# Values of all tokens projected token-major in the first stage of an attention block, and the nine projections that are left in a step in another order

## What is computed

```python
x = x + attn(layernorm(x), ...)
q = (h @ Wq.T).reshape(B, L, H, D)          # H = 32 heads, D = 128
k = (h @ Wk.T).reshape(B, L, KVH, D)        # KVH = 8 groups, 4 heads each
v = (h @ Wv.T).reshape(B, L, KVH, D)
q, k = rope(q), rope(k)
dt = softplus(h @ Win.T + dt_bias); g = dt * -exp(A_log_bias)
G = cumsum of g inside chunks of 128 tokens
y = (q k^T * decay(G)) (v dt)  +  (q exp(G)) state      # four chunks of 128 tokens
state = state * exp(G_last) + (k exp(G_last - G))^T (v dt)
y = rmsnorm(y) * silu(h @ Wg.T)             # the gates
out = y @ Wo.T
```

## Time and profile before

| what | value |
|---|---|
| median of three runs | 1900.76 us (1895.67 to 1905.22) |
| the profiled execution, its own time | 1901.62 us |
| its span, first to last instruction | 1899.8 us |
| TensorE busy | 1825.1 us, 96% |
| VectorE, ScalarE, GpSimd busy | 67%, 36%, 34% |
| first scores of step 0 | 75.59 us |
| first scores of step 31, the last | 1355.05 us |
| mean granted TensorE clock | 0.985 |

### The profile page before, as it was taken

The page is one execution under the profiler, slowest core; times in us unless marked ns, Lnnn a source line. Parts: engine busy times, 40 slices in busy tenths (PEclk is TensorE's granted clock), DMA queues, the critical chain, the costliest instruction groups (busy, mean ns, idle before and its releaser), DMA issues. The chain is left out here.

```text
span 1899.8 us, 27788 instructions
## 1 busy us (share of the span) xinstructions
PE 1825.1 (96%) x8856; PEld 1480.4 (78%) x8856; DVE 1272.5 (67%) x2340; ACT 692.9 (36%) x2186; POOL 646.0 (34%) x741
## 2 busy tenths in 40 slices
PE   6799999999999999999999999999889999999997
PEld 5578888787887888787788878888667888888885
DVE  7777877787787878787777867887755333333332
ACT  4433444443344444334344433443443211212111
POOL 3444444444444444444443444444401011010110
PEclk9899999999999999999999999999989999999998
DMA  4132332233333223323322332322465232322321
GB/s 156 45 106 73 99 101 66 71 98 100 82 92 96 75 65 107 100 79 84 95 74 65 106 89 82 91 64 76 130 197 165 68 100 82 96 85 80 100 80 32
DMA packets 111073, 173.54 MB, mean 91 GB/s; under 512 B 8016, under 2 KB 45904, under 8 KB 110928
## 3 DMA queue, kind: packets, MB, share of 16 engines
q1 hardware_dynamic: 110928, 171.80, 30.3%
HBM read 133.50 MB, written 38.27 MB: 90 GB/s over the span
## 5 line engine op out<-in xcount | busy, mean ns | idle before, releaser
L84 PE MATMUL p_proj<-wg_hi,shared 128*128 128x512 f32 x1024 | 360.7, 433 | 0.0
L84 PE MATMUL p_proj<-shared,wq_hi 128*128 128x512 f32 x992 | 335.4, 399 | 0.0
L113 POOL TENSOR_TENSOR q<-rope_a,rope_b 128x512 f32<-128x512 f32 x128 | 166.4, 1300 | 344.8 <-DVE rope_b L105 211.7
L84 PEld LDWEIGHTS p_proj<-wg_hi,shared 128*128 128x128 f32 x1024 | 193.6, 189 | 84.9 <-issue 40.7
L917 ACT ACTIVATE tanh<-p_proj 128x512 f32<-128x512 f32 x128 | 76.6, 598 | 444.4 <-PE p_proj L84 444.4
L84 PEld LDWEIGHTS p_proj<-shared,wq_hi 128*128 128x128 f32 x992 | 186.4, 188 | 44.7 <-issue 1.7
L84 PE MATMUL p_proj<-wg_lo,shared 128*128 128x512 f32 x512 | 203.0, 396 | 0.0
L84 PE MATMUL p_proj<-shared,wq_lo 128*128 128x512 f32 x496 | 196.0, 395 | 0.0
L910 ACT ACTIVATE probs<-g_row,stab 128x128 f32<-128x128 f32 x512 | 164.0, 402 | 53.7 <-POOL g_row L1024 53.7
L694 PE MATMUL p_y<-v_tok,probs 128*128 128x128 f32 x1024 | 182.1, 275 | 0.0
L84 PE MATMUL p_proj<-shared,wkv_hi 128*128 128x512 f32 x496 | 172.0, 408 | 0.0
(11 more groups left out here) (181 smaller groups left out, 3755.4 us busy)
## 6 DMA issues: line engine op xcount, KB each, us to landing
g_row<-g_scratch SPq DMA_DIRECT2D x128, 256.0 KB, 6.0
z_scratch<-z_st SPq DMA_DIRECT2D x256, 128.0 KB
w_raw<-z_scratch SPq DMA_DIRECT2D x63, 512.0 KB, 6.6
e_row<-e_scratch SPq DMA_DIRECT2D x96, 256.0 KB, 3.9
w_raw<-in_wq_t SPq DMA_DIRECT2D x16, 512.0 KB, 7.9
w_raw<-in_wg_t SPq DMA_DIRECT2D x16, 512.0 KB, 5.4
w_raw<-in_wo_t SPq DMA_DIRECT2D x11, 512.0 KB, 7.2
w_raw<-in_wkv_t SPq DMA_DIRECT2D x8, 512.0 KB, 5.0
```

The source lines that it names most:

```text
L84: mm = pe.matmul(out, lhs[a], rhs[e], start=(i == 0 and j == 0), stop=(i == len(pairs) - 1 and j == 2))
L113: pool.tensor_tensor(out, keep["rope_a"][:, s, :], keep["rope_b"][:, s, :], ALU.add).then_inc(keep["roped"], 1)
```

## The change

The values of all tokens and groups are computed in `norm_stage`: there are 32 products `values(v)` of 12 matmuls each, v = 0 to 15 for the first four groups (one for each token tile) and 16 to 31 for the others, with the tokens on the output's partitions. ScalarE saves each (`save_v`) and SyncE stores it to a scratch tensor in memory (`v_scratch`). In the attention stage SyncE loads the values of the next step by one DMA at a step's start (`load_v`). V_UNIT, `v_turn`, `v_t` and the two copies on ScalarE are gone. The nine units left stand in a new order in the step, with the banks in turn. VectorE and GpSimd each make the low part of one half of the query and gate weights, where VectorE made both.

```diff
@@ norm_stage, SyncE
+            for i in (1, 2):
+                sp.dma_start(part(w_raw, i), half_piece(io["wv_t"], 0, i)).then_inc(wv_in[0], 16)
+            sp.dma_start(win[:, :, :], io["win_t"].rearrange("(k p) h -> p k h", p=P)).then_inc(win_in, 16)
             load_x(1)
+            load_x(2)
+            load_x(3)
@@ norm_stage, VectorE
-                    if i == 11:
-                        dve.wait_ge(trig_in, 32)
-                        rotate_tile(0)
+                    if i == V_LAG:
+                        for h in (1, 2):
+                            dve.wait_ge(w_hi, h)
+                            dve.tensor_tensor(dst(wv[0][1], h), part(w_raw, h), dst(wv[0][0], h).bitcast(F32),
+                                              ALU.subtract).then_inc(wv_lo, 1)
@@ norm_stage, TensorE
-            pe.wait_ge(small_in, 16 * (1 + 2 * B))
+            def values(v):
+                half, i = v // NT, v % NT
+                if i == 0:
+                    if half:
+                        pe.wait_ge(w_lo, 2)
+                    else:
+                        pe.wait_ge(wv_lo, 2)
+                pe.wait_ge(lo_set, i + 1)
+                if v >= 2:
+                    pe.wait_ge(v_set, v - 1)
+                wide(pe, pv[v % 2][:, :], [(x_parts(keep, i // NC, kt, slice(i % NC * P, (i % NC + 1) * P)),
+                                            (wv[half][0][:, kt, :], wv[half][1][:, kt, :])) for kt in range(KT)]).then_inc(v_done, 1)
...
             for i in range(NT):
                 turn(i)
                 if i:
                     dt_rows(i - 1)
+                if i >= V_LAG:
+                    values(i - V_LAG)
             dt_rows(NT - 1)
-            pe.wait_ge(w_lo, 3)
-            for h in range(HG):
-                project_q(h)
+            for v in range(NT - V_LAG, NT + TABLES_AT):
+                values(v)
             for k in (T_BIAS, T_W):
                 turn_table(k)
+            for r in range(ROPED):
+                project_tile(r)
+                values(NT + TABLES_AT + r)
+            for v in range(NT + TABLES_AT + ROPED, 2 * NT):
+                values(v)
@@ attention_stage
-        K_UNIT, V_UNIT, Q_UNIT, GATE_UNIT = 0, 9, (2, 4, 6, 7), (1, 3, 5, 8)
+        K_UNIT, Q_UNIT, GATE_UNIT = 0, (1, 3, 5, 6), (2, 4, 7, 8)
-        BANKS = (0, 1, 2, 1, 0, 2, 1, 0, 2, 1)
+        BANKS = (0, 1, 2, 0, 1, 2, 0, 1, 2)
@@ attention_stage, SyncE
             def step(g, b, n):
+                if ahead(n):
+                    if has_last(n):
+                        sp.wait_ge(y_done, NC * n)
+                    else:
+                        sp.wait_ge(keep["v_out"], 16 * 2)
+                    load_v(g + (b + 1) // B, (b + 1) % B)
                 for c in range(NC):
@@ attention_stage, TensorE
             def step(g, b, n):
                 scores(n, 0)
                 next_unit(g, b, n, K_UNIT)
                 chunk_state(n, 0)
+                next_unit(g, b, n, Q_UNIT[0])
                 gates(g, b, n, 0)
-                mix(n, 0)
-                for c in (1, 2):
-                    scores(n, c)
-                    next_unit(g, b, n, Q_UNIT[c - 1])
-                    chunk_state(n, c)
-                    gates(g, b, n, c)
-                    mix(n, c)
+                mix(g, b, n, 0)
+                scores(n, 1)
+                next_unit(g, b, n, Q_UNIT[1])
+                chunk_state(n, 1)
+                gates(g, b, n, 1)
+                mix(g, b, n, 1)
+                scores(n, 2)
                 next_unit(g, b, n, Q_UNIT[2])
+                chunk_state(n, 2)
+                next_unit(g, b, n, Q_UNIT[3])
+                mix(g, b, n, 2)
                 scores(n, 3)
-                next_unit(g, b, n, Q_UNIT[3])
+                gates(g, b, n, 2)
                 gates(g, b, n, 3)
                 if ahead(n):
                     k_turn(n + 1, b + 1)
-                next_unit(g, b, n, V_UNIT)
-                mix(n, 3)
-                if ahead(n):
-                    v_turn(n + 1)
+                mix(g, b, n, 3)
@@ attention_stage, GpSimd
                 row_landed(n, 3)
                 if ahead(n):
-                    add_rope(pool, keep, n + 1, b + 1, 1)
+                    add_rope(pool, keep, n + 1, b + 1, 2)
                 mask(n, 3)
                 rms(n, 1)
                 if ahead(n):
+                    add_rope(pool, keep, n + 1, b + 1, 3)
                     row_landed(n + 1, 0)
                     step_tables(g if b < B - 1 else g + 1, (b + 1) % B, n + 1)
-                    add_rope(pool, keep, n + 1, b + 1, 2)
                     mask(n + 1, 0)
+                    row_landed(n + 1, 1)
+                    add_rope(pool, keep, n + 1, b + 1, 4)
                 rms(n, 2)
                 if ahead(n):
-                    add_rope(pool, keep, n + 1, b + 1, 3)
-                    row_landed(n + 1, 1)
-                    add_rope(pool, keep, n + 1, b + 1, 4)
                     mask(n + 1, 1)
```

More of the change, by code:

```diff
@@ L172, in x_part, with v_place, v_count @@
             return shared[:, b * KT:(b + 1) * KT, e, c * P:(c + 1) * P]
+        TABLES = 4
+        V_LAG, TABLES_AT = 3, 9
+        def v_place(v):
+            if v >= 2 * NT - 2:
+                return (keep["k"][:, 1, :], v_tok[:, 1, :, :].rearrange("p c d -> p (c d)"))[v - (2 * NT - 2)]
+            return xin[:, v, :] if v < NT - 2 else v_rows[v % 4]
+        early_out, place_out = sem("n_early_out"), [sem(f"n_place_out{i}") for i in range(4)]
+        def v_count(v):
+            return early_out if v < NT - 2 else place_out[v % 4] if v < 2 * NT - 2 else v_out
         @block.sync
@@ L363, in _ @@
             act.activation(eg[:, :], G[:, :], ACT.Exp).then_inc(eg_set, 1)
+            for v in range(NT + 4, NT + TABLES_AT):
+                save_v(v)
+            w_high(wg, 1, g_in, 32)
+            w_high(wg, 2, g_in, 32)
             for j, k in enumerate((T_BIAS, T_W)):
@@ L366, in _ @@
                 act.activation(tab[:, :, k, :], ptab[k][:, :, :], ACT.Copy).then_inc(tabs_saved, 1)
+            for v in range(NT + TABLES_AT, 2 * NT):
+                save_v(v)
         @block.tensor
@@ L546, in first @@
             def first():
+                load_v(0, 0)
                 load_g(0, 0, 0)
@@ L855, in step @@
                 make_state(n, b, 0)
+                rotate_next(g, b, n, Q_UNIT[0], 1)
                 make_gate(g, b, n, 0)
                 if group_ahead(g) and b == B - 2:
[L858 to L870 removed]
+                    k_low_weights(g + 1)
@@ new lines, in step @@
+                make_probs(n, 1)
+                scale_q(g, b, n, 1)
+                q_low(n, b, 2)
+                make_z(n, 0)
+                opening_lows(n, (2, 3))
+                rotate_next(g, b, n, Q_UNIT[1], 2)
+                turn_z(n, 0)
+                make_state(n, b, 1)
+                make_gate(g, b, n, 1)
+                make_probs(n, 2)
+                scale_q(g, b, n, 2)
+                q_low(n, b, 3)
+                make_z(n, 1)
+                opening_lows(n, (4, 5))
@@ L871, in step @@
                 rotate_next(g, b, n, Q_UNIT[2], 3)
+                turn_z(n, 1)
+                make_state(n, b, 2)
+                rotate_next(g, b, n, Q_UNIT[3], 4)
                 make_probs(n, 3)
                 scale_q(g, b, n, 3)
+                if ahead(n):
+                    k_low(n + 1, b + 1)
+                make_gate(g, b, n, 2)
+                if ahead(n):
+                    q_low(n + 1, b + 1, 0)
                 make_z(n, 2)
                 opening_lows(n, (6, 7))
-                rotate_next(g, b, n, Q_UNIT[3], 4)
+                if group_ahead(g) and b == B - 2:
+                    q_low_weights(g + 1)
```

359 lines of the change are left out of this document (185 added, 174 removed).

## The result

The changed kernel takes 2034.89 us (median of 4 runs, 2026.73 to 2036.81) against 1902.74 (1895.67 to 1905.22, one run more than in the table ahead): a ratio of 1.070, 95% interval 1.067 to 1.072. It is slower by 7%. The profiled execution took 2026.73 us, at the fast end of the runs, with a span of 2024.9.

A forecast was written before the change was run, and what follows sets the result against it. TensorE's own work was taken to bound the step. First stage +77.5, steps +13.6 and clock +67 on 1899.8 gave a span of 2057.9, and 2059 us for the execution; likeliest range 2035 to 2085, whole range 1960 to 2100.

The forecast's parts named there:

- First stage: Stage before the first scores: the values' matmuls moved in make it 153 us against 75.59, +77.5 us.
- The chain of tables: First stage: the tables' log and exponential chain lies beside 33.6 us of values; bare, it adds up to 20.
- rival 3: First stage bound by something else, such as tables or stores: up to 20 us more, 2079 with the clock's fall; chance 0.05.
- A step without waits: Attention step: without the V unit and the turn, TensorE's work falls from 40.35 to 37.1 us.
- The step n = 27: Step of the kernel before: at 40.95 us, already as long as the chain from e_row to the next scores.
- The chain: State, e_row, stores, row, last add, q_lo, scores: steps of 40.9 us, 44.5 in seven b = 0; +13.6 us.
- Weight splits at nothing: Shared splits move 1.2 us from VectorE to GpSimd in two steps of four, beside TensorE's work, at no cost.
- The clock: Steps behind stalls: TensorE's clock falls after 27 of 31 stalls, 2.5 us each, +67 us.
- Rival 1: Steps: the clock stays up, 1992 us, or 1975 to 2035 with a few falls; chance 0.20.
- Rival 2: Steps: the row is not late, each takes 37.1 us, and the time is 1849 us; chance 0.13.
- Its deciding point: Row's landing: the last add must start by 34.2 us in the step, so e_row must go out by 24.2.

The follow-up runs named there:

- experiment 1: The changed kernel with SyncE loading the row (n + 1, 1) ahead of the state wait, the e_row load and four stores: 1844.99 us, 0.970 of the kernel before.
- experiment 3: The kernel before the change, with the row (n + 1, 1) loaded ahead of the state wait, e_row load and stores: 1876.68 us, ratio 0.987.
- experiment 6: The changed kernel with the row (n + 1, 1) issued right behind the e_row load, ahead of the four stores and query weights: 1845.12 us, ratio 0.971.
- experiment 4: The changed kernel with 12 unread matmuls (24 in some steps b = 0) filling TensorE's stall, the row still late: 1997.62 us.
- 5b: The changed kernel with TensorE's stall filled by unread matmuls and all weight splits on VectorE, none on GpSimd: 1988.60 us.
- 5a: The changed kernel with all weight splits on VectorE, none on GpSimd, the stall not filled: 2034.73 us.
- experiment 7: The changed kernel with the row (n + 1, 1) ahead of the query weights but behind the stores, in seven steps b = 0 only: 2019.76 us.

## Why the prediction held, and which terms were off

The forecast was 2059 us, with a likeliest range of 2035 to 2085; 2034.89 lies 0.1 below that and inside the whole range. It lies as well in the range of the rival whose clock stays up "with a few falls", 1975 to 2035, so the number alone would not have told the two apart; the 26 falls in the trace do. Against the predicted span of 2057.9 the profiled one is 33.0 shorter: 3.8 of it in the first stage, 24.6 in the steps, 4.6 in the rest. The median then lies 10.0 above that span, where I had added 0.9.

*First stage, right.* Predicted 153 us, measured 149.3. The first values start at 20.38, where I had about 20; TensorE is busy for 133.7, where I had 135. What I over-counted is mostly idle time; and my own terms, 135.4 busy and 18.5 idle, add up to 153.9, not 153. The chain of tables was covered; rival 3 fell.

```profile
9.41 1.94 PE L445 MATMUL n_pt<-ident,n_xn 128*128 128x128 f32 x8 [9.41 <-DVE n_xn L297]
...
20.38 0.73 PE L85 MATMUL p_tok<-wg_hi,shared 128*128 128x512 f32 x2
```

*A step without waits, right.* 37.1 predicted, 37.09 in experiment 1.

*The step n = 27, misread.* I took its 40.95 us for a step already as long as its chain. In experiment 3 the row is early and the steps b = 3 are still 40.9 to 41.0 long, so the row did not set them; TensorE waits 0.3 us for xw in each of them, with the row early or late. The lengths that I took from that step, 9.99 and 2.87 us, don't hang on this.

*The chain, right in mechanism and nearly in size.* Experiments 1 and 6 show that the row's place on SyncE is the cause: either edit alone ends the stall. Its terms can be read in experiment 4, where the clock is out of the way: e_row at 28.04 in an ordinary step (predicted 28.06), the add 9.7 to 10.2 later (9.99), 2.83 to the scores (2.87). Steps b = 1 and b = 2 are 40.4 to 41.0 (40.9), but for two that began at the lower clock. The steps' sum there is 1306.1, where I had 1293.1. Of the missing 13 us, 12 are the steps b = 3, 42.0 instead of 40.9, and b = 0, 45.1 instead of 44.5.

*Weight splits at nothing, wrong in part.* I named TensorE's work as their cover and a price of 1.2 to 2.5 us in 14 steps if it failed. What I missed is GpSimd's queue: behind a late add the split of 2.4 us holds up the next xw. That step failed because I counted an engine's free time in a step and not where in the step the free time lies. The saving failed too: I had 1.2 us of VectorE's work moving to GpSimd with each share, but VectorE's half took 2.7 to 3.3 us beside GpSimd's, and its busy time did not fall (982.2 and 979.2). The shared split costs 5 to 9 us with the clock up (4 against 5b); in the changed kernel itself undoing it gave nothing that its runs could show (5a).

*The clock, right in kind, too large in size.* I took 27 falls of 2.5 us, +67. There were 26 falls, close to it. TensorE's busy time in the steps is 1205.54, against 1151.71 in experiment 1 for the same matmuls: 53.8 us, 2.1 for each fall. And not all of it reaches the end: keeping the clock up gave back 29 us in the steps of the trace, 37 by the medians (experiment 4). Of the 29, some 27 are in the steps b = 1 and b = 2, and next to nothing is in the steps b = 3, where the state is late for GpSimd's queue anyway, and b = 0, where the cause is open. What I wrote of it, "A loss early in a step also delays its state, so the next stall is as long again", holds only for b = 1 and b = 2. All these counts are of the fastest of the four executions; the other three read a mean clock of 0.952 to 0.953, not 0.959, and took 8 to 10 us more, so the count of 26 is that of one execution. By the Trainium skill (TensorE: Matmul & The Clock Gate, HAM oscillation), in the kernel that it describes every burst behind such a wait starts at half rate. The trace agrees on the level, 0.51 over the first 3 us of the step n = 15, and not on every one: 5 of 31 started at full clock.

*Rival 1* (the clock stays up, 1992) fell in this kernel; experiment 4, 1998, is nearly its number. *Rival 2* (the row not late, 1849) didn't happen, but its number was the useful one: once the row is early the kernel takes 1845. Its deciding point, an add that starts by 34.2, agrees with experiment 6, where it starts at 33.13 in the step n = 15 and TensorE doesn't wait; in the step n = 16 it starts at 34.60, and TensorE waits 0.07 us.

In the steps the two errors had opposite signs: the chain's part was 13 us too small and the clock's 38 too large, by the traces' 29. That they partly cancel is luck; without experiment 4 the sum would have looked like a single small miss.

*The rest of the program.* It took 544.8 us in the profile before and 540.1 after. In experiment 3, where that part is the old program, it took 1872.7 - 1333.2 = 539.5, so this is scatter between executions, not the change.

## What to carry to other kernels

Before taking work away from the bounding engine, look for the chain that arrives only just behind that work: here the wait of a side engine for a 256 KB row (4.83 us in the earlier trace rows) was visible and harmless in that step before, and set the step afterwards. On an issue queue, put what is needed soonest ahead of what nobody waits for: one load moved past a wait and four stores turned 7% slower into 3% faster. And a wait moved further down an in-order engine's queue is not removed: it holds whatever comes next (136 us of 190 by moving the add, all of it by moving the load).

## What the runs showed of the hardware

The length of a stall alone didn't tell whether the clock fell. Stalls of 1.92, 2.79 and 2.94 us were followed by the lower level; stalls of 3.02, 3.10, 3.21, 3.27 and 3.43 were not, and two others of 3.27 were. Other traces widen the overlap: in experiment 4 stalls of 2.09 and 2.50 us were followed by the lower level and one of 2.43 was not, and in experiment 7 one of 3.65 was not. What else decides is open; I made no experiment on it. In a step that began at the lower level TensorE was busy for 1.5 to 3.0 us more than its 37.1.

The same subtraction of 128x1024 on VectorE took 1.20 to 1.58 us without a split on GpSimd beside it (experiments 1 and 5a), and 2.7 to 3.3 us while GpSimd did the other half of the same weights (experiments 1 and 4 and the changed kernel). So sharing a split between the two took nothing off VectorE's busy time here. Why the two halves slow each other, or whether it is only VectorE's that is slowed, no run shows.

The length of a GpSimd operation varies: the same xw of 128x512 took 1.03 us in one place and 2.02 in another of the same kernel (experiment 4). I saw this only in the timeline and didn't isolate it.
